# Score masks on VectorE instead of TensorE, evacuations spread over ScalarE and GpSimd, and an expert phase without a score table

## The reference, cut to what matters

```python
x = _layernorm(x + _L0_attn_ref(...))    # grouped queries, 16 heads of 32, 4 of k and v; mask of ones and zeros ADDED
x = _layernorm(x + _L0_xattn_ref(...))   # latent cross attention on ctx
x = _layernorm(x + _L0_ffn_ref(...))     # ternary weights
x = _layernorm(x + _L1_attn_ref(...))    # decay attention, no softmax
x = _layernorm(x + _L1_xattn_ref(...))   # causal cross attention, 16 heads of 32
x = _layernorm(x + _L1_ffn_ref(...))     # 8 experts, 2 of them per token, and a shared FFN
```

```python
scores = jnp.einsum('btkgd,bskd->bkgts', qg, k) * scale
scores = scores + jnp.tril(jnp.ones((T, T)))[None, None, None]      # first attention
p = jax.nn.softmax(scores, axis=-1)
...
scores = jnp.where(causal, scores, jnp.finfo(scores.dtype).min)     # causal cross attention
...
topk_w, topk_idx = jax.lax.top_k(jax.nn.softmax(x @ gate_weight.T), 2)
y = jnp.einsum('tef,te,ehf->th', act, combine, down_weights)        # act = silu(gate) * up
```

## Time and profile before

| | |
|---|---|
| time, median of 3 (lowest, highest) | 2093.61 us (2092.49, 2094.29) |
| the profiled execution: its own time, its span | 2087.5 us, 2085.7 us |
| busy: PE, DVE, ACT, POOL | 90%, 50%, 34%, 18% |
| gqa, causal phase | about 0 to 267, 1297 to 1531 us |
| shared, expert phase | about 1531 to 1752, 1772 to 2086 us |
| mean granted TensorE clock | 0.967 of 2.4 GHz |

### The profile page before, as it was taken

How to read it: one execution, slowest core, us unless ns; L and a number is a source line. 1 busy time by engine, 2 the same in 40 slices (tenths; PEclk the granted TensorE clock), 3 DMA queues, 4 the chain that set the end, 5 groups by cost and what they waited for, 6 DMA issues and landing times. The chain is left out here.

```text
span 2085.7 us, 32789 instructions
## 1 busy us (share of the span) xinstructions
PE 1887.3 (90%) x12124; PEld 1535.6 (74%) x12124; DVE 1041.1 (50%) x1836; ACT 713.2 (34%) x2275; POOL 385.6 (18%) x339
## 2 busy tenths in 40 slices
PE   8899888999999989999899998899879995999991
PEld 6667566788888767777677776677658874899990
DVE  5666753455555446333364547677865332222224
ACT  3555624334444332111231102545632210233332
POOL 1111100000000038000021100001104322745335
PEclk9999999999999999999999999999999998999995
DMA  7110142000000022000093000000015100644257
GB/s 238 42 46 14 43 160 82 1 1 1 1 1 1 1 76 91 1 0 0 24 352 115 1 20 27 26 2 1 2 46 207 46 0 0 243 149 143 82 114 205
DMA packets 73375, 135.89 MB, mean 65 GB/s; under 512 B 13456, under 2 KB 31760, under 8 KB 71184
## 3 DMA queue, kind: packets, MB, share of 16 engines
q1 hardware_dynamic: 47376, 96.28, 13.3%
q0 software_dynamic: 7888, 27.94, 4.5%
q10 hardware_dynamic: 17968, 9.71, 1.8%
HBM read 90.62 MB, written 43.29 MB: 64 GB/s over the span
## 5 line engine op out<-in xcount | busy, mean ns | idle before, releaser
L1473 PE MATMUL banks<-ternary_xth,ternary_wq 128*128 (+1 forms) x352 | 140.6, 399 | 5.0 <-DVE ternary_wq L1404 3.6
L1473 PE MATMUL banks<-ternary_xtl,ternary_wq 128*128 (+1 forms) x352 | 139.4, 396 | 0.0
L97 PE MATMUL banks<-latent_vh,latent_cth 128*128 128x512 f32 x256 | 104.2, 407 | 3.5 <-DVE latent_ctl L1174 3.5
L97 PE MATMUL banks<-weights,expert_xgh 128*128 x312 | 104.7, 336 | 2.4 <-DVE expert_xgl L2086 2.4
L99 PE MATMUL banks<-weights,expert_xgl 128*128 x312 | 101.6, 326 | 0.0
L573 ACT ACTIVATE gqa_pr<-banks,gqa_nb 128x128 f32<-128x128 f32 x256 | 90.4, 390 | 32.6 <-DVE gqa_nb L715 32.6
L98 PE MATMUL banks<-weights,expert_xgh 128*128 x312 | 101.4, 325 | 0.0
L573 ACT ACTIVATE causal_pr<-banks,causal_nb 128x128 f32<-128x128 f32 x256 | 90.4, 395 | 31.1 <-DVE causal_nb L715 31.1
L99 PE MATMUL banks<-latent_vh,latent_ctl 128*128 128x512 f32 x256 | 100.1, 391 | 0.0
L98 PE MATMUL banks<-latent_vl,latent_cth 128*128 128x512 f32 x256 | 100.1, 391 | 0.0
L1433 DVE TENSOR_TENSOR ternary_hf<-ternary_sg,banks 128x512 f32<-128x512 f32 x44 | 30.2, 687 | 135.4 <-issue 79.5
(11 more groups left out here) (462 smaller groups left out, 5412.0 us busy)
## 6 DMA issues: line engine op xcount, KB each, us to landing
x_slots<-decay_zeros SPq DMA_DIRECT2D x39, 256.0 KB, 4.3
y_slots<-decay_zeros SPq DMA_DIRECT2D x39, 256.0 KB, 4.5
y_slots<-expert_ys SPq DMA_DIRECT2D x39, 256.0 KB
expert_xin<-x_slots SPq DMA_DIRECT2D x38, 256.0 KB, 2.9
weights_raw<-in_expert_experts SPq DMA_DIRECT2D x4, 2176.0 KB, 9.2
gqa_tw<-in_ternary_w ACTq DMA_DIRECT2D x4, 2112.0 KB
ternary_raw<-in_ternary_w SPq DMA_DIRECT2D x11, 768.0 KB, 4.1
expert_raw<-in_expert_experts POOLq DMA_DIRECT2D x3, 2176.0 KB, 9.7
```

Source lines behind the costliest of these rows:

```text
L97: pe.matmul(out, wh, xh, start=first, stop=False, **kw)
L1473: a = pe.matmul(dst[:, :], wq[:, j, m, c * P:(c + 1) * P], x[:, c, toks], start=c == 0 and n == 0, stop=c == C - 1 and n == 1)
```

## The change

In gqa and causal attention:

- The mask products on PE go. DVE adds the mask (`tril` or `causal`, broadcast over eight heads) to the scores and writes them to `pr` in SBUF; it takes the maxima there, and ACT makes the exponentials in place. PE's next scores wait for the mask add (`masked`), not for the exponentials.
- q leaves PSUM on ACT, with a bias scaled beforehand (`bqs`). The second copy of the transposed exponentials (half 1) is on ACT too (`pt_late`); half 0 stays on DVE. The low half `otl` is made by POOL.
- In `plan`, `lo` and `rec` stand ahead of the scores, half 1's transposes right behind them, and the second mask add and maximum ahead of the slot's projections, but for batches 0, 4 and 8.

In the shared and expert phase:

- The score scatter, its table and the loads from it are gone. y is written unscaled. The low gathers are plain, two in flight, and DVE adds both gathers times the score with one multiply-add each; the high gathers wait for the low adds.
- The x transposes of tiles 1 to 38 are in fp32r, with a rounded identity.

```diff
         for b in range(B + 2):
             for h in range(2):
+                if soft and h == 0 and b >= 2:
+                    plan.append(("lo", b - 2, 0))
+                if soft and h == 0 and 1 <= b <= B:
+                    plan.append(("rec", b - 1, 0))
                 if b < B and (h == 0 or not soft):
                     plan.append(("S", b, h))
-                if soft and h == 0 and b >= 2:
-                    plan.append(("lo", b - 2, 0))
+                if soft and h == 0 and 1 <= b <= B:
+                    plan.append(("T", b - 1, 1))
+                with_x = b % GT == 0 and b < B - GT
+                if soft and h == 0 and b < B and not with_x:
+                    plan.append(("S", b, 1))
                 if b < B - GT:
                     plan += [(n, b // GT + 1, i) for n, i in by_slot[2 * (b % GT) + h]]
                 elif kind == "decay" and b < B:
                     plan += [(n, 0, i) for n, i in next_slots[2 * (b % GT) + h]]
-                if soft and h == 0 and b < B:
+                if soft and h == 0 and b < B and with_x:
                     plan.append(("S", b, 1))
...
         for k, e in enumerate(act_plan):
             j = k
-            while e[0] in ("x", "c", "nx", "nc") and act_plan[j - 1][0] in ("S", "lo"):
+            while (e[0] in ("x", "c", "nx", "nc") and act_plan[j - 1][0] in ("S", "lo") or
+                   e[0] == "T" and act_plan[j - 1][0] == "S" or
+                   soft and e[0] == "q" and act_plan[j - 1][0] == "S" and act_plan[j - 1][2] == 1):
                 act_plan[j], act_plan[j - 1] = act_plan[j - 1], act_plan[j]
                 j -= 1
...
         banked = [e for e in plan if e[0] in ("x", "c", "q", "k", "v", "rt", "pv", "out", "nx", "nc", "nq", "nk", "nv")]
         place = {e: k for k, e in enumerate(banked)}
-        by_act = [e for e in banked if e[0] == "rt" or kind == "decay" and e[0] == "k"]
+        by_act = [e for e in banked if e[0] == "rt" or e[0] == ("q" if soft else "k")]
         by_dve = [e for e in banked if e not in by_act]
         act_frees = {e: k + 1 for k, e in enumerate(by_act)}
...
                     by_head = rec[:, b % 2, :].rearrange("p (r j) -> p j r", j=4).unsqueeze(3).broadcast_to((P, 4, 4, D))
                     pool.tensor_copy(spread[:, :].rearrange("p (j r d) -> p j r d", r=4, d=D), by_head).then_inc(spread_done, 1)
+                elif what == "lo":
+                    pool.wait_ge(oth_done, b + 1)
+                    pool.tensor_tensor(out=otl[:, b % 2, :], in0=on[:, b % 2, :], in1=f32(oth[:, b % 2, :]),
+                                       op=ALU.subtract).then_inc(otl_done, 1)
                 elif what == "out" and b < normed_here:
                     pool.wait_ge(ve_done, b + 1)
...
                     if what == "v":
                         constants()
-                if what == "k" and e in act_frees:
+                if what == "q" and e in act_frees:
+                    act.wait_ge(pp_full, place[e] + 1)
+                    if kind == "gqa":
+                        act.wait_ge(biases_done, 1)
+                        act.activation(qt[:, b % 2, h, :], bank_of(e), ACT.Identity, bias=bqs[:, h:h + 1],
+                                       scale=scale).then_inc(free_a, 1)
+                    else:
+                        act.activation(qt[:, b % 2, h, :], bank_of(e), ACT.Copy, scale=scale).then_inc(free_a, 1)
+                elif what == "T" and h == 1:
+                    act.wait_ge(pt_full, 2 * b + 2)
+                    if kind == "gqa" and b == 1:
+                        act.wait_ge(ws_lo, 3)
+                    act.activation(pt[:, b % 2, 8:16, :], unit_banks(2), ACT.Copy).then_inc(pt_late, 1)
+                elif what == "k" and e in act_frees:
                     act.wait_ge(pp_full, place[e] + 1)
                     act.activation(kt[:, b % 2, h, :], bank_of(e), ACT.Identity,
...
                     u = 2 * b + h
                     act.wait_ge(max_done, u + 1)
-                    if u >= 2:
-                        act.wait_ge(pt_full, u - 1)
-                    elif kind == "gqa":
-                        act.wait_ge(ws_lo, 2)
...
                 elif what == "S" and soft:
                     dve.wait_ge(s_full, b + 1)
-                    dve.tensor_reduce(nb[:, h, :], unit_banks(h), AX, ALU.max, negate=True).then_inc(max_done, 1)
+                    if u >= 2:
+                        dve.wait_ge(pt_full, u - 1)
+                    elif kind == "gqa":
+                        dve.wait_ge(S.loaded, 16 * len(S.tables))
+                        dve.wait_ge(ws_lo, 2)
+                    dve.tensor_tensor(pr[:, h, :, :], unit_banks(h), mask, ALU.add).then_inc(masked, 1)
+                    dve.wait_ge(masked, u + 1)
+                    dve.tensor_reduce(nb[:, h, :], pr[:, h, :, :], AX, ALU.max, negate=True).then_inc(max_done, 1)
...
                     dve.wait_ge(kr_hi, 1)
                     dve.tensor_tensor(S.ahead.krl[:, :], S.ahead.kr, f32(S.ahead.krh[:, :]), ALU.subtract).then_inc(kr_lo, 1)
-                elif what == "T":
+                elif what == "T" and h == 0:
                     dve.wait_ge(pt_full, u + 1)
                     if kind == "gqa" and u == 2:
                         dve.wait_ge(ws_lo, 3)
-                    dve.tensor_copy(pt[:, b % 2, 8 * h:8 * h + 8, :], unit_banks(2)).then_inc(pt_done, 1)
+                    dve.tensor_copy(pt[:, b % 2, 0:8, :], unit_banks(2)).then_inc(pt_done, 1)
                 elif what == "rec":
                     dve.wait_ge(exp_done, 2 * b + 2)
...
                 elif what == "pv" and soft:
                     dve.wait_ge(free_a, act_frees[("rt", b, 0)])
+                    if b >= 2:
+                        dve.wait_ge(otl_done, b - 1)
                     dve.tensor_tensor(on[:, b % 2, :], bank, rts[:, :], ALU.mult).then_inc(free_d, 1)
                 elif what == "pv":
...
                     if h == 1:
                         continue
-                    if u == 0 and soft:
-                        pe.wait_ge(const_hi, 2)
                     if u % 8 == 0 and not (kind == "causal" and b == 0):
                         wait_freed(pe, ("q", b // GT, C - 1))
                         wait_freed(pe, ("k", b // GT, nk - 1))
                     if b >= 1:
-                        pe.wait_ge(exp_done if soft else pt_done, u)
-                    if soft:
-                        for r in range(4):
-                            pe.matmul(S.bank[r], identr[:, :], maskr[:, :].unsqueeze(1).broadcast_to((P, 4, P)),
-                                      start=True, stop=False)
+                        pe.wait_ge(masked if soft else pt_done, u)
                     for j in range(4):
                         for r in range(4):
...
                             k = kt[rows, b // GT % 2, j if nk > 1 else 0, tokens(b)]
                             dst = S.bank[r][:, j * P:(j + 1) * P]
-                            if soft:
-                                m = pe.matmul(dst, q, k, start=False, stop=j == 3)
-                            else:
-                                m = pe.matmul(dst, k, q, start=True, stop=True)
+                            lhs, rhs = (q, k) if soft else (k, q)
+                            m = pe.matmul(dst, lhs, rhs, start=True, stop=True)
                     m.then_inc(s_full, 1)
                 elif what == "T":
                     pe.wait_ge(exp_done, u + 1)
-                    if u >= 1:
-                        pe.wait_ge(pt_done, u)
+                    if h == 1:
+                        pe.wait_ge(pt_done, b + 1)
+                    elif b >= 1:
+                        pe.wait_ge(pt_late, b)
                     for c in range(8):
                         m = pe.transpose(S.bank[4 + c // 4][:, (c % 4) * P:(c % 4 + 1) * P], pr[:, h, c, :], S.ident[:, :])
...
                 if t % GT == GT - 1:
                     pool.wait_ge(scattered, 16 * 2 * (t + 1))
-            for n in range(2 * B):
-                at = bass.IndirectOffsetOnAxis(ap=S.pos[:, n:n + 1], axis=0)
-                if n and n % 2 == 0:
-                    pool.wait_ge(scored, 16 * n)
-                pool.indirect_dma_start(S.s_slots, at, S.score[:, n:n + 1], None).then_inc(scored, 16)
-            pool.wait_ge(scored, 16 * 2 * B)
         @block.scalar
...
             landed(E - 2)
             for t in range(B):
-                pool.indirect_dma_start(S.X[:, t, :], None, S.y_slots, slots(t), compute_op=ALU.add).then_inc(low_added[t], 16)
+                if t >= 2:
+                    pool.wait_ge(low_in[t - 2], 16)
+                pool.indirect_dma_start(yg[t], None, S.y_slots, slots(t)).then_inc(low_in[t], 16)
             pool.wait_ge(y_out[(TILES - 1) % 2], 16 * ((TILES - 1) // 2 + 1))
             for t in range(B):
+                pool.wait_ge(low_added, t + 1)
                 pool.indirect_dma_start(yg[t], None, S.y_slots, slots(B + t)).then_inc(yg_in[t], 16)
```

(20 more changed lines are left out.)

71 lines of the change are left out of this document (24 added, 47 removed).

## The result

The changed kernel takes 2076.24 us (median of 5 runs, 2072.92 to 2082.82), the kernel before 2092.64 (2090.37 to 2094.29): a ratio of 0.9924, 95% interval 0.9905 to 0.9944. It is faster, by 16.4 us where I forecast 33.5, and outside my range of 2046 to 2074. The changed kernel's profiled execution took 2076.24 us (span 2074.4). The profiled execution of before, from which the sum was made, was 5 us under its median, so the traces differ by 11.3 us and the medians by 16.4.

What follows compares the result with a forecast made beforehand. PE, busy 90% of the span, was taken as the bound. Gqa -12, causal -4, phase change -16.5, tiles -2 and tail +1 sum to -33.5: 2087.5 to 2054.0, plus 6.1 for the median gives 2060 us, range 2046 to 2074.

Steps and rivals of the forecast that it cites:

- The sixteen exponentials ... end ACT's round at 12 us: Gqa batches 0 to 11: exponentials, q and magnitude pass end ACT's round at 12 us, inside the 13.3 us batch.
- Batch 1 gives 2.3: Gqa batch 1: 2.3 us less, since its queue of copies on DVE was late too.
- batch 1 gives 3.5: Causal attention's batch 1, which ran in a half-clock stretch before: 3.5 us less.
- Together +2: Gqa's last four batches: added mask add and slower low half on POOL cost 2 us together.
- the last four ... 0.9: Causal attention's last four batches, without magnitude pass: 0.9 us less.
- rival 5: Attention batches: PE waits for DVE's mask, add and maximum, clock falls each time; +51, 2111 us; 0.04 with sums of mishaps.
- rival 4: Between shared and expert phase: something else holds the phase change, say at 1767; +11, 2071 us; 0.15 shared with rival 2.
- rival 3: Expert tiles: fp32r transposes are slower, +15.7, 2078 us, or load-free, 2054; chance 0.13 shared with rivals 1 and 6.
- The tail: After the last tile: multiply-adds and paired low gathers move the last add to about 2075, +1 us, bounds 0 to +3.
- Rival 1: All 32 attention batches: POOL's low half and DVE stretch each other by 0.6 us; +19, 2079; 0.13 with rivals 3, 6.
- Rival 2: Attention: v order and ACT round cost more, causal gives nothing, gqa half; +10, 2070 us; 0.15 shared with rival 4.
- Rival 6: Attention: no gain because DVE takes over as bound; phase end, tiles and tail left, 2076 us; 0.13 with rivals 1, 3.

Runs made afterwards that it cites:

- PSUM form: Changed kernel, but DVE writes the masked scores back into their PSUM banks, and maxima and exponentials read PSUM: 2069.51 us, ratio 0.9898.
- x first: Changed kernel, but in batch 0 of gqa and causal attention DVE makes x's low halves ahead of the first mask add and maximum: 2080.45 us, ratio 0.9945.
- fillers: Changed kernel with 8 useless products ahead of each of the last five output products of both attention phases: 2073.16 us, ratio 0.9905.
- v first: Changed kernel, but in causal batches 3, 7 and 11 the v entries stand between the two maxima again: 2079.21 us, ratio 0.9943.
- attention alone: Kernel before with only the attention part of the change, shared and expert phases as before: 2108.46 us, ratio 1.0091.
- expert side: Kernel before with only the shared and expert part of the change, attention as before: 2065.65 us, ratio 0.9885.
- three order and clock edits: Changed kernel with x first, v first and fillers together: 2068.45 us, ratio 0.9879; on the PSUM form: 2056.85 us, ratio 0.9840.
- tail edit: DVE takes eight of sixteen low-row multiply-adds before the last tile; on the changed kernel 2074.57 us (0.9919), on PSUM form plus three order and clock edits 2054.15 (0.9827).

## Why the prediction was wrong

**The full gqa batches: right.** I forecast 13.3 us from 14.65 and got 13.5 in four of six (13.95 and 14.14 in the others), and 13.28 once the exponentials were short. That PE's mask work leaves its path one for one, and that masks, maxima and copies hide, was the right reading. Six batches gave 5.6 us of 7.9.

**"The sixteen exponentials ... end ACT's round at 12 us": the first step that failed.** I carried over the duration that they have from PSUM. From SBUF they are 0.04 us farther apart, 0.64 us a batch, and the round ends at 13.0 us, in a loop where many projection batches wait for it. gqa's batches 0, 2, 3, 7 and 11, forecast at -4.0, came to +0.6; the three causal k batches, forecast at -0.5, to +2.3. The PSUM form gave back 10.5 us in both phases, of which 3.25 in causal batch 1 are no matter of the exponentials' pace alone. The Trainium skill's "VectorE: DVE Perf Modes" (The TRN2 errata) gives ScalarE a fixed term of 224 cycles from SBUF and 172 from PSUM at 1.2 GHz, an estimate of 43 ns more per instruction from SBUF; the traces agree, with 40 ns.

**"Batch 1 gives 2.3" and "batch 1 gives 3.5": wrong, about 11 us with batch 0.** I saw that today's copies were late there and took the rest as free. DVE now has a mask add on top of the maximum ahead of two of the first x low halves, PE waits 3.0 and 3.5 us for them instead of 1.7, and works at half clock behind that (0.54 in the causal window above). gqa's batches 0 and 1 came to +0.6 together, the causal ones to +4.6. x first gave back 0.9 and 1.3 us of it. Moving the weights' split did not: the wait went to ACT. The 7.13 us wait of causal batch 1 was only split or moved to another engine by the edits.

**"Together +2" and "the last four ... 0.9" at the ends: mis-sized.** They cost +6.4 in gqa and +4.6 in causal attention. The smaller part lies in the loop that I had added up (10.97 us forecast, 9.0 to 12.6 measured; three periods together +1.6 us in gqa, -0.8 in causal attention), the larger behind the last score product: from there to the next phase gqa takes 31.7 us instead of 26.9, causal attention 33.7 instead of 28.3. There PE waits 1.5 to 3.6 us for each low half, where it was 0.9 to 2.3, and the clock falls in these gaps: fillers give back 4.8 us. This is rival 5's mechanism, which I priced in the causal v gaps alone. In both phases together the clock fell from 0.97 to 0.93 over 467 us of windows, an estimate of at most 19 us, 12 of rival 5's stretches, if all of it lay on the path; how much did, beyond what the fillers gave, no run shows.

**The v batches: gap right, cost a little under.** PE stands idle 3.19 us for v in each, as forecast, and the three batches cost +6.5 us where I had +2.8 and 2 for the clock. v first showed that closing the gaps gives 2.6 us of that, since ACT's reciprocals stand right behind it.

**Phase change and tiles: right.** -18.5, half a microsecond past my bounds of -14 to -18 (taken -16.5): with the score scatters gone, 1.5 us are left between DVE's last add and the next phase, and rival 4 is out. The transposes gave 2.8 us where I had 2, neither rival 3's loss nor its gain.

**The tail: +1 had the sign right in most executions and missed the held-up gather.** The profiled execution's -2.3 is the exception; with the held-up gather it is +2.4 to +4. Rival 1 looked for DVE and POOL in each other's way in the attention batches, where no row shows it (mask adds 1.22 us, low halves 1.28). It is likely here, in sixteen adds with two SBUF operands over a gather's issue: all twelve held-up issues end with the block, and none is held up in the two traces with the block broken up. It is not shown to the end, since three executions with the whole block escaped it, I can't say why, and the medians moved too little. The Trainium skill's "GPSIMD Engine Reference" (Key points) names DVE operations with two SBUF inputs among those that contend with GpSimd; twelve of these fifteen traces agree.

**The 6.1 us added for the median** was a property of one execution: the changed kernel's profiled run is its median. By the trace of before alone I would have said 2054, farther off.

**The rivals.** Rival 2, "the v order and the ACT round cost more than I think", named the place and priced it at 10 us, where 29 were missing. Rival 6 has the number that came, 2076, by luck: it takes attention as unchanged because DVE bounds it, but full batches did gain 1.1 us, attention alone ran 16 us slower, and the expert side gained 26.6 by medians where rival 6 had 17.5.

In sum, of the 29 us missing in attention (forecast -16, measured +13.4), the PSUM form and three order and clock edits bring back 22.4 in the traces. Alone, the PSUM form moved the ratio most (0.9898 from 0.9924), and even there the intervals overlap; the other three are read from single traces, and shown by medians only together. About 7 us, in the first two batches of both phases and in the v batches, stay unexplained. Also open is why the changed kernel's five runs spread over 10 us and the four of the PSUM form over 1.3; with the tail edit four spread over 7.

## What to carry to other kernels

When work moves to another engine, price again every operation whose operand changes its memory, not only those that move: sixteen small ones at 40 ns each can fill the slack that the move was to live from. Read a loop's first and last rounds by themselves, with their waits and their clock, since an edit that pays in full rounds can lose it all there. A long block of additions on VectorE is better kept away from GpSimd's gathers, though here that is likely and not proven.

## What the runs showed of the hardware

An exponential of 128 columns takes 0.385 us from SBUF and 0.345 from PSUM, while DVE's mask add of 128x1024 takes 1.22 us whether it writes SBUF or PSUM. A transpose of a 128x128 float32 block costs 0.02 us less in fp32r (0.077 for four). Behind a wait of 3.47 us PE's products ran at a granted clock of 0.54 over 7 us, behind one of 1.74 us in the kernel before at 1.00. Overwritten products in 2 to 4 us gaps kept the granted clock at 1.00 in place of 0.86 at gqa's end, and that phase and causal attention were 2 to 3 us shorter; where PE waited for a bank instead of an operand they cost 2.8 us and more. And one indirect gather's issue on GpSimd, 0.95 us otherwise, took 4.1 to 6.8 us in twelve of fifteen executions and ended each time 0.82 us behind VectorE's block of additions.
